# Receptance projection of the steady loop in seven half-width products

## The reference, cut to what matters

```python
x_prev = jnp.pad(x[:, :-1, :], ((0, 0), (1, 0), (0, 0)))
xk = x * time_mix_k + x_prev * (1.0 - time_mix_k)          # likewise xv, xr
k = jnp.einsum('btd,ed->bte', xk, W_k)
v = jnp.einsum('btd,ed->bte', xv, W_v)
r = jax.nn.sigmoid(jnp.einsum('btd,ed->bte', xr, W_r))
wkv = _wkv_scan(k, v, time_decay, time_first)              # exp-weighted recurrence over time
y = r * wkv
x = x + jnp.einsum('btd,ed->bte', y, W_o)
# FFN on layernorm(x): 256 -> 1024 (two, gated) -> 1024 -> 1024 -> 256
h = jax.nn.silu(_tlin(h0, w1_w, w1_s)) * _tlin(h0, w2_w, w2_s)
h = jax.nn.gelu(_tlin(h, h1_w, h1_s), approximate=False)
h = jax.nn.gelu(_tlin(h, h2_w, h2_s), approximate=False)
x = x + _tlin(h, w3_w, w3_s)
```

## Time and profile before

| | us |
|---|---|
| time, median of 3 runs | 1485.84 (1485.73 to 1486.19) |
| the profiled execution's own time | 1485.31 |
| its span, first to last instruction | 1483.6 |
| PE busy | 1473.6 (99%) |
| DVE busy | 1205.3 (81%) |
| ACT busy | 1077.1 (73%) |
| POOL busy | 204.3 (14%) |

### The profile page before, as it was taken

How to read it: one execution, slowest core, us unless ns; L and a number is a source line. 1 busy time by engine, 2 the same in 40 slices (tenths; PEclk the granted TensorE clock), 3 DMA queues, 4 the chain that set the end, 5 groups by cost and what they waited for, 6 DMA issues and landing times.

```text
span 1483.6 us, 28137 instructions
## 1 busy us (share of the span) xinstructions
PE 1473.6 (99%) x10326; PEld 1324.7 (89%) x10326; DVE 1205.3 (81%) x1554; ACT 1077.1 (73%) x1626; POOL 204.3 (14%) x173
## 2 busy tenths in 40 slices
PE   8999999999999999999999999999999999999999
PEld 6989898998989989899898989989899898998998
DVE  7797887868888687887878878788886878878655
ACT  6895776867768777686867868677587776868655
POOL 1314020110201102011030210202011020110200
PEclk9999999999999999999999999999999999999999
DMA  9977474755737467374674746657475673746654
GB/s 352 380 264 270 148 231 118 222 160 171 242 97 242 125 204 227 106 248 117 203 210 130 235 130 205 176 168 227 103 240 139 193 234 97 250 117 201 192 178 140
DMA packets 94926, 285.28 MB, mean 192 GB/s; under 512 B 9136, under 2 KB 33328, under 8 KB 92976
## 3 DMA queue, kind: packets, MB, share of 16 engines
q1 hardware_dynamic: 86736, 277.01, 57.5%
q0 software_dynamic: 8160, 7.87, 4.5%
HBM read 250.76 MB, written 33.03 MB: 191 GB/s over the span
## 4 chain that ended last, share of the span: by engine, by line
PE 93%; DVE 3%; ACT 2%; issue 1%; POOL 1%; DMA 0%; DVEq 0%; POOLq 0%; ACTq 0%
PE acc L645 27%; PE acc L647 26%; PE att L554 10%; PE acc L619 7%; PE acc L620 7%; PE acc L671 4%; PE acc L673 4%; PE att L577 3%; PE att L533 2%; PE att L620 1%; PE att L619 1%; DVE stage L1724 1%; DVE op_lo L1595 0%; PE acc L773 0%; PE acc L771 0%
## 5 line engine op out<-in xcount | busy, mean ns | idle before, releaser
L645 PE MATMUL acc<-op_hi,ring 128*128 128x256 f32 x3360 | 810.7, 286 | 0.5 <-issue 0.5
L647 PE MATMUL acc<-op_lo,ring 128*128 128x256 f32 x3360 | 788.8, 279 | 0.0
L645 PEld LDWEIGHTS acc<-op_hi,ring 128*128 128x128 f32 x3360 | 632.2, 188 | 18.6 <-issue 17.6
L647 PEld LDWEIGHTS acc<-op_lo,ring 128*128 128x128 f32 x3360 | 632.0, 188 | 11.1 <-issue 10.0
L1595 DVE TENSOR_TENSOR op_lo<-blocks,op_hi 128x1024 fp32r<-128x1024 f32 (+2 forms) x271 | 338.9, 1265 | 98.3 <-ACT op_hi L1007 90.9
L1007 ACT ACTIVATE op_hi<-blocks 128x1024 fp32r<-128x1024 f32 (+2 forms) x263 | 283.7, 1091 | 82.8 <-DVE blocks L1590 74.9
L619 PE MATMUL acc<-x_hi,w_rnd 128*128 128x512 f32 x420 | 167.6, 399 | 0.0
L620 PE MATMUL acc<-x_lo,w_rnd 128*128 128x512 f32 x420 | 165.9, 395 | 0.0
L2018 POOL TENSOR_TENSOR v_sb<-mix_v,v_sb 128x1024 f32<-128x1024 f32 (+1 forms) x19 | 39.4, 2072 | 833.7 <-DVE r_sb L1522 824.8
L1047 ACT ACTIVATE blocks<-acc,vec 128x256 f32<-128x256 f32 x268 | 104.9, 475 | 60.9 <-PE acc L647 60.8
L1047 ACT ACTIVATE blocks<-parts,vec 128x256 f32<-128x256 f32 x240 | 102.3, 497 | 56.2 <-DVE parts L1652 47.9
(11 more groups left out here) (185 smaller groups left out, 2116.8 us busy)
## 6 DMA issues: line engine op xcount, KB each, us to landing
ring<-scratch SPq DMA_DIRECT2D x427, 512.0 KB, 4.2
scratch<-stage SPq DMA_DIRECT2D x11, 1024.0 KB, 12.4
stage<-in_w_ffn SPq DMA_DIRECT2D x10, 1024.0 KB, 10.9
x_in<-in_x SPq DMA_DIRECT2D x32, 256.0 KB, 4.8
out<-x_next SPq DMA_DIRECT2D x30, 256.0 KB, 5.1
out<-mix_v POOLq DMA_DIRECT2D x30, 256.0 KB, 4.4
scratch<-in_w_ffn SPq DMA_DIRECT2D x4, 1024.0 KB, 15.0
ring<-stage SPq DMA_DIRECT2D x7, 512.0 KB, 9.4
```

The source lines that it names most:

```text
L645: pe.matmul(out, act(w), act(op_hi[:, k, c, :]), start=(begins and c == 0 and m % 2 == 0), stop=False, skip_group_check=True)
L647: mm = pe.matmul(out, act(w), act(op_lo[:, k, c, :]), start=False, stop=(c == QC - 1), skip_group_check=True)
```

## The change

The receptance r of tile i+1 is a 2x2 block product: two output chunks, two input chunks, two sequences. Before, it is 8 block products of 128x256 (chunks 4 and 5, each two products of 512 columns). After, it is 7, with sums of weight blocks (made once before the loop, on POOL) and sums of mixed inputs (four differences on DVE in every pass). ACT copies three intermediate results, DVE adds two more, and the exponential of r is done in three pieces. The seven products stand at four points (`r_point`) in PE's loop. To free banks 6 and 7, chunk 3 of the projection (the last of v) is moved from behind step 2 to behind step 5, and its copy on ACT from behind `p5` to behind `g12`. On DVE, `gain` moves behind `t1b`. On ACT, the fourth `exp` moves ahead of `hiT23`.

```diff
+        wr_sums = sb("wr_sums", [P, 4, P])
...
+        wr11, wr12, wr21, wr22 = (wm[:, 2, c, e * P:(e + 1) * P] for e in range(2) for c in range(2))
+        r11, r12, r21, r22 = (mix_r[:, c, n * SEG:(n + 1) * SEG] for c in range(2) for n in range(2))
+        r_t1, r_t2, r_t3, r_t4 = (x1_next[:, k, :] for k in range(4))
+        R_X, R_Z, R_Y = BANK[6][:, 0:SEG], BANK[7][:, 0:SEG], BANK[7][:, SEG:2 * SEG]
...
+            def r_point(t, k):
+                u = t - 2
+                if k == 0:
+                    pe.wait_ge(WHOLE.dve_mix.sem, WHOLE.dve_mix.at(t))
+                    pe.wait_ge(WHOLE.act_kvr.sem, WHOLE.act_kvr.at(t, 2 * DC))
+                    pe.wait_ge(dve_tr.sem, dve_tr.at(u, 1))
+                    r_matmul(R_Z, wr_s1, r_t1, True, False)
+                    pe_r.add(r_matmul(R_Y, wr11, r11, False, False))
+                if k == 1:
+                    pe.wait_ge(act_r.sem, act_r.at(u, 2))
+                    pe.wait_ge(dve_tr.sem, dve_tr.at(u, 3))
+                    WHOLE.pe_kvr.add(r_matmul(R_X, wr_s2, r_t2, False, False))
+                    mm = r_matmul(R_Y, wr12, r21, False, True)
+                    pe_r.add(mm)
+                if k == 2:
+                    pe.wait_ge(act_r.sem, act_r.at(u, 3))
+                    pe.wait_ge(WHOLE.act_kvr.sem, WHOLE.act_kvr.at(t, 2 * DC + 1))
+                    WHOLE.pe_kvr.add(r_matmul(R_X, wr_s3, r_t3, False, False))
+                    pe_r.add(r_matmul(R_Z, wr_s4, r22, False, True))
+                if k == 3:
+                    pe.wait_ge(dve_r.sem, dve_r.at(u, 1))
+                    pe.wait_ge(dve_tr.sem, dve_tr.at(u, 4))
+                    pe_r.add(r_matmul(R_X, wr22, r_t4, False, True))
...
                     step(i, 0, 1)
                     project(WHOLE, i + 1, [0, 1, 2])
-                    step(i, 0, 2, [0])
-                    step(i, 0, 2, [1])
-                    project(WHOLE, i + 1, [3])
+                    step(i, 0, 2)
                     step(i, 0, 3)
                     step(i, 0, 4)
                     step(i, 0, 5)
-                    project(WHOLE, i + 1, [4])
-                    step(i, 0, 6)
+                    project(WHOLE, i + 1, [3])
+                    step(i, 0, 6, [0])
+                    r_point(i + 1, 0)
+                    step(i, 0, 6, [1])
                     step(i, 1, 0, [0])
-                    project(WHOLE, i + 1, [5])
+                    r_point(i + 1, 1)
                     step(i, 1, 0, [1])
+                    r_point(i + 1, 2)
                     step(i, 1, 1)
+                    r_point(i + 1, 3)
                     step(i, 1, 2)
...
                 p5(i, 0)
-                copy_kvr(WHOLE, i + 1, [3])
                 hi6(i)
                 u2(i, 0)
...
                 g12(i, 0)
+                copy_kvr(WHOLE, i + 1, [3])
                 g22(i, 0)
                 hiB22(i)
                 hiT1(i)
-                copy_kvr(WHOLE, i + 1, [4])
+                r_copy(i + 1, 0)
+                r_copy(i + 1, 1)
                 g21(i, 0)
+                exp(WHOLE, i + 1, 3)
+                r_copy(i + 1, 2)
+                r_exp(i + 1, 0)
                 hiT23(i)
-                exp(WHOLE, i + 1, 3)
                 p1(i, 1)
                 hiB21(i)
-                copy_kvr(WHOLE, i + 1, [5])
-                exp_r(WHOLE, i + 1)
+                r_exp(i + 1, 1)
+                r_exp(i + 1, 2)
...
                 clamps(WHOLE, t)
                 lo6(i)
                 loB11(i)
+                r_difference(t, 0)
+                r_difference(t, 1)
                 c12(i, 0)
-                gain(WHOLE, t)
+                r_difference(t, 2)
+                r_difference(t, 3)
                 c22(i, 0)
                 t1b(i)
+                gain(WHOLE, t)
...
                 loB22(i)
+                r_sum(t, 0)
+                r_sum(t, 1)
                 loT23(i)
```

More of the change, by code:

```diff
@@ L254, in build @@
         LAST_BLOCK = BANK[6][:, 0:D]
+        wr11, wr12, wr21, wr22 = (wm[:, 2, c, e * P:(e + 1) * P] for e in range(2) for c in range(2))
+        wr_s1, wr_s2, wr_s3, wr_s4 = (wr_sums[:, k, :] for k in range(4))
+        r11, r12, r21, r22 = (mix_r[:, c, n * SEG:(n + 1) * SEG] for c in range(2) for n in range(2))
+        r_t1, r_t2, r_t3, r_t4 = (x1_next[:, k, :] for k in range(4))
+        r_p5, r_u2 = r_t1, r_t2
+        R_X, R_Z, R_Y = BANK[6][:, 0:SEG], BANK[7][:, 0:SEG], BANK[7][:, SEG:2 * SEG]
+        r_out = [[r_sb[:, e, n * SEG:(n + 1) * SEG] for n in range(2)] for e in range(2)]
         PAIR_OF, ALL = (slice(0, 2), slice(2, 4)), slice(0, QC)
@@ L347, in build @@
         ld_ring = [tally(f"ld_ring{k}", USES, 16) for k in range(SLOTS)]
+        pe_r, act_r, dve_r, dve_tr = (tally(n, k, ahead=0) for n, k in (("pe_r", 4), ("act_r", 3), ("dve_r", 2), ("dve_tr", 4)))
+        sum_r = ctx.enter_context(nc.semaphore("sum_r"))
         ld_x = tally("ld_x", n_seq, 16)
@@ L556, in project, with r_matmul @@
                     s.pe_kvr.add(mm)
+            def r_matmul(out, w, x, start, stop):
+                return pe.matmul(out, w, x, start=start, stop=stop, skip_group_check=True)
+            def r_point(t, k):
[21 more added lines that the diff above has]
+                    pe_r.add(r_matmul(R_X, wr22, r_t4, False, True))
             def project_out(s, t):
@@ L828, in mlp @@
                 pe.sem_inc(pe_half.sem, HALF_STEPS - PLAIN_STEPS)
+                pe.wait_ge(sum_r, 4)
                 with pe.Fori(1, NT - 1) as i:
@@ L965, in exp_r, with r_copy, r_exp @@
                 s.act_exp.add(act.activation(r_sb[:, :, s.cols], r_sb[:, :, s.cols], ACT.Exp, scale=-1.0))
+            def r_copy(t, k):
+                act.wait_ge(pe_r.sem, pe_r.at(t - 2, (1, 1, 2)[k]))
+                dst, src = ((R_X, R_Y), (r_p5, R_Z), (r_u2, R_X))[k]
+                act_r.add(act.activation(dst, src, ACT.Copy))
+            def r_exp(t, k):
+                if k == 0:
+                    act.wait_ge(pe_r.sem, pe_r.at(t - 2, 2))
+                    WHOLE.act_kvr.add(act.activation(r_out[0][0], R_Y, ACT.Exp, scale=-1.0))
+                if k == 1:
+                    act.wait_ge(pe_r.sem, pe_r.at(t - 2, 4))
+                    WHOLE.act_kvr.add(act.activation(r_out[1][0], R_X, ACT.Exp, scale=-1.0))
+                if k == 2:
+                    act.wait_ge(dve_r.sem, dve_r.at(t - 2))
+                    late_half = by_seq(r_sb[:])[:, :, 1, :]
+                    WHOLE.act_exp.add(act.activation(late_half, late_half, ACT.Exp, scale=-1.0))
             def seed_x(s, t):
+                if s is WHOLE and not isinstance(t, int):
+                    act.wait_ge(dve_r.sem, dve_r.at(t - 2))
                 act.wait_ge(s.act_kvr.sem, s.act_kvr.at(t))
@@ L1441, in first_running_max, with r_difference, r_sum @@
                 link(s, dve.tensor_copy(carry_p[:, :, s.seqs], seq[:, :, s.seqs, SEG:SEG + 1]))
+            def r_difference(t, k):
+                if k == 0:
+                    dve.wait_ge(WHOLE.dve_mix.sem, WHOLE.dve_mix.at(t))
+                    dve.wait_ge(st_x1.sem, st_x1.at(t - 1))
+                if k == 2:
+                    dve.wait_ge(dve_tr.sem, dve_tr.at(t - 2, 1))
+                if k == 3:
+                    dve.wait_ge(dve_tr.sem, dve_tr.at(t - 2, 3))
+                dst, a, b = ((r_t1, r12, r11), (r_t3, r22, r12), (r_t2, r22, r_t1), (r_t4, r21, r_t2))[k]
+                dve_tr.add(dve.tensor_tensor(dst, a, b, ALU.subtract))
+            def r_sum(t, k):
+                dve.wait_ge(pe_r.sem, pe_r.at(t - 2, 3))
+                dst, a, b = ((r_out[1][1], R_X, r_p5), (r_out[0][1], R_Z, r_u2))[k]
+                dve_r.add(dve.tensor_tensor(dst, a, b, ALU.add))
             def now_exponents(s, t):
@@ L1493, in gain @@
                 dve.wait_ge(s.act_exp.sem, s.act_exp.at(t, 2))
+                if s is WHOLE:
+                    dve.wait_ge(s.act_kvr.sem, s.act_kvr.at(t, 2 * DC))
                 if s is FIRST[0]:
@@ L1520, in gated_denominator @@
                 dve.wait_ge(s.act_exp.sem, s.act_exp.at(t))
+                if s is WHOLE:
+                    dve.wait_ge(s.act_kvr.sem, s.act_kvr.at(t))
                 settle(s, t)
@@ L2067, in _, with r_weights @@
             pool.sem_inc(WHOLE.pool_chain.sem, WHOLE.pool_chain.per)
+            def r_weights(k, dst, a, b, subtract):
+                if k:
+                    pool.wait_ge(sum_r, k)
+                pool.tensor_tensor(dst, a, b, ALU.subtract if subtract else ALU.add).then_inc(sum_r, 1)
+            r_weights(0, wr_s1, wr21, wr22, False)
+            r_weights(1, wr_s2, wr_s1, wr11, True)
+            r_weights(2, wr_s3, wr11, wr21, True)
+            r_weights(3, wr_s4, wr12, wr_s2, True)
             tile_deviation(1, 1)
```

## The result

| | before | after |
|---|---|---|
| median of 4 runs, us | 1485.78 (1485.54 to 1486.19) | 1654.08 (1653.67 to 1654.91) |
| ratio, 95% interval | | 1.1132 [1.1119, 1.1145] |
| one pass of the loop, mean of 14 | 90.36 | 102.41 |

What follows compares the result with a forecast made beforehand. PE was taken to bound the kernel, busy for all 90.37 us of a pass. Terms -0.42 + 0.18 + 9.13 + 0.28 + 2.1 = 11.27 us per pass, 157.8 us over 14 passes, gave 1643 us, range 1609 to 1661.

Steps and rivals of the forecast that it cites:

- the clock stays up: Rival: the clamp's wait ahead of step 6 is there but PE's clock does not fall; 1613.7 us, chance 0.12.
- the main case: All five terms together, with the clamp's wait and a clock fall in every pass: 1643 us, 1630 to 1660, chance 0.77.
- The products, -0.42: Receptance on PE: 14 half-width matmuls replace 8 full ones, 3.02 against 3.44 us, 0.42 us less per pass.
- Step 4, +0.18: PE reaches step 4 1.72 us sooner and waits for `p5` to copy bank Z; 0.18 us per pass, 0 to 0.3.
- The clamp, +9.13: DVE's clamp over mix_v waits for the moved chunk, delaying `c22` and PE's step 6; 9.13 us per pass, 8.8 to 9.5.
- Point 2, +0.28: PE waits at point 2 for ACT's chain behind step 6, 4.85 against 4.60 us; 0.28 us per pass, 0 to 0.7.
- The clock, +2.1: PE's clock falls in the gap ahead of step 6; each restart costs 2.1 us per pass, 0 to 3.4.
- The rule drawn on: For PE's gap ahead of step 6: an idle array falls back to the halved clock, and only activity releases it.
- The mean granted clock of a pass: Sign in the changed profile: PE's granted clock averages 0.98 over a pass.
- The clamp's wait does not bind: Rival: DVE's clamp is not held up and the seven products save their 0.42 us per pass; 1479.4 us, chance 0.015.
- only ACT's chain binds: Rival: without the clamp's wait, only ACT's chain to point 2 delays PE, 0.15 us per pass; 1487.4 us, chance 0.01.
- The 0.57 us: Lateness of ACT's chain to point 2 without the clamp's wait, in place of 0.28 plus 0.18, in a rival.

Runs made afterwards that it cites:

- The version with all waits covered: Changed kernel with clamp into k_sb, chunk 2 behind step 3, fourth exponential behind `hiT23`, r's first exponential replaced by copy and later exponential: 1482.87 us, ratio 0.9983.
- the run with the cover: Changed kernel with the clamp into k_sb and chunk 2 of the projection behind step 3: 1487.15 us, ratio 1.0008.
- the one without: Changed kernel with only the clamp written to k_sb instead of mix_v, denominator and reciprocals going to mix_v: 1490.71 us, ratio 1.0028.
- the filled gap: Changed kernel with nine more products, results unused, on PE between chunk 3 and step 6: 1618.28 us, ratio 1.0878.
- the case of 7.05 us: Kernel before, eight full products kept, with only chunk 3 moved behind step 5 and its copy behind `u2`: 1610.61 us, ratio 1.0838.
- gap of 5.4 us: Changed kernel with chunk 3 one step earlier, behind step 4 instead of step 5: 1599.16 us, ratio 1.0747.
- the one with the late table load: Changed kernel with the clamp into k_sb and ACT's fourth exponential behind `hiT23`: 1493.86 us, ratio 1.0049.

## Why the prediction was right

It forecast 1643 us with 1609 to 1661, and 1654.08 came. The range is wide since it also holds the case in which the clock stays up; the main case had 1630 to 1660. By its steps, per pass:

- **The products, -0.42.** Right: a product of 256 columns (two matmuls) takes 0.43 us; where the clamp writes elsewhere, the two of point 1 start at 826.34 and 826.77. The version with all waits covered gains 0.26 of it.
- **Step 4, +0.18.** Right cause, a little small: 0.27, and 0.28 by the run with the cover against the one without. Behind a wait the second matmul too starts 0.07 late, which the step did not count.
- **The clamp, +9.13.** Right: 705.97 - 695.15 - 1.72 = 9.10. The four differences have 1.46 of it, as the sum had. `c12` started 11.3 us behind step 4, and the gap came in 14 of 14 passes.
- **Point 2, +0.28.** Right: 0.24. The chain is the one it named: in the rows of ACT above, `g21` starts at 713.58, the load, the fourth exponential and the copy follow, the exponential of r ends at 718.08, and PE goes at 718.13. What it didn't say is that the load stands there because of the fourth exponential, and that without it the load would stand behind ACT's wait for point 1.
- **The clock, +2.1.** The mechanism was right and the size was not: 2.7 by the filled gap. The sum was made from the 20 slow matmuls at the start of the kernel, 4.4 us of work; behind each gap 5.7 to 5.9 us of work were slow. (The trace holds no granted clock ahead of 6.2 us, so that the level at the start is read from the spacing alone.) The rule drawn on (the Trainium skill, TensorE: Matmul & The Clock Gate, part 1) is borne out: the idle array went to the halved clock, some 4.7 us into the wait, and came back only behind work; an idle of 1.2 us in the filled gap did not bring it down. The row at the start wasn't a stand-in for the price: the runs have 1.4, 2.5 and 2.7 us per fall. The mean granted clock of a pass, expected at 0.98, was 0.95, as the clock was low over 4.4 us of idle time as well.

Measured terms: -0.42 + 0.27 + 9.10 + 0.24 + 2.7 = 11.9 of the 12.05; the forecast had 11.27. Of the 11 us between forecast and result, 8 to 9 are the clock's term and 1 is step 4's. Of the missing 0.15 per pass, 0.1 is described at the end; the rest is open.

Of the rivals, "the clock stays up" (1613.7) is what the filled gap made real, at 1618. "The clamp's wait does not bind" (1479.4) and "only ACT's chain binds" (1487.4) needed another buffer for the clamp; with one, the kernel comes out at 1490.7, since both the wait at step 4 (0.27) and the one at point 2 (0.30 there) then remain and together take more than the 0.42. The 0.57 us that the second of them gives for ACT's chain has no working in the text; what was measured is 0.57 for the two waits together.

## What to carry to other kernels

Before moving a piece of work later on one engine, list the operations that overwrite its operands and see where they stand in the other engines' lists: an overwrite is a wait like a read, and in an in-order list it holds up everything behind it. A wait on TensorE of 5 us or more cost 1.4 to 2.7 us beyond its length here, on average over the passes. And an operation that seems to be in the way may be doing a service, such as a table load during someone else's wait, or covering the step that follows.

## What was not expected of the hardware

- The price of a fall of the clock depends on when it comes. With gaps of 9.1, 7.6, 7.05 and 5.4 us it cost 2.7, 2.2, 1.4 and 2.5 us per pass: part of the slow stretch lies in the idle time, where it is free, and in the case of 7.05 us that was most of it (of the slow stretch from 885.2 to 892.0 only 2.8 us were work). With one and the same gap of 5.4 us it cost from 1.4 to 3.1 us, as the clock fell between 2.5 and 4.7 us into the wait and came back behind 2.9 to 6.2 us of work.
- A gap of 5.4 us already brings the fall; idle times of 1.2 us (the filled gap) and 1.4 us (chunk 3 back in its place) did not. Between these no run lies.
- In some stretches the matmuls of 256 columns stand 0.118 us apart and not 0.1167, at a granted clock of 1.00: in the version that gains, the 112 between point 3 and the output projection take 13.38 us, where in the one with the late table load they take 13.26. Over a whole pass the mean spacing is 0.1168 us before, 0.1170 after the change and 0.1172 with the clamp in k_sb, which makes some 0.1 us for the 430 matmuls of a pass. Its cause is open; no experiment was made on it.
